# Planes of the experts' weight pieces, worked two slots later in the second attention

## The reference

```
h = _layernorm(x, ln1_g, ln1_b)
q = (h @ Wq).reshape(Bb, Ss, H, Dh); k = ...; v = ...
scores = jnp.einsum('bqhd,bkhd->bhqk', q, k) / jnp.sqrt(jnp.float32(Dh))
ctx = jnp.einsum('bhqk,bkhd->bqhd', jax.nn.softmax(scores, axis=-1), v)
x = x + ctx @ Wo
m = _layernorm(x, ln2_g, ln2_b)
probs = jax.nn.softmax(m @ Wg, axis=-1)
wts, idx = jax.lax.top_k(probs, K)
h1 = jax.nn.gelu(jnp.einsum('td,edf->etf', xt, W1) + b1[:, None, :])
ye = jnp.einsum('etf,efd->etd', h1, W2) + b2[:, None, :]
```

## Time and profile before

| | |
|---|---|
| median of 3 runs | 2354.14 us (2352.45 to 2356.22) |
| the profiled execution | 2354.95 us |
| its span | 2353.2 us |
| mean granted clock of TensorE | 0.904 |
| PE busy | 1868.1 us, 79% |
| DVE busy | 1611.5 us, 68% |
| ACT busy | 1474.4 us, 63% |

### The profile page before, as it was taken

The page is one execution under the profiler, slowest core; times in us unless marked ns, Lnnn a source line. Parts: engine busy times, 40 slices in busy tenths (PEclk is TensorE's granted clock), DMA queues, the critical chain, the costliest instruction groups (busy, mean ns, idle before and its releaser), DMA issues. The chain is left out here.

```text
span 2353.2 us, 39104 instructions
## 1 busy us (share of the span) xinstructions
PE 1868.1 (79%) x12343; PEld 1137.1 (48%) x12344; DVE 1611.5 (68%) x3496; ACT 1474.4 (63%) x2762; POOL 593.1 (25%) x638
## 2 busy tenths in 40 slices
PE   3577787878787877857998988898774699999990
PEld 1344554545454544532333333332223588888880
DVE  4488888888888888856766666666625555555556
ACT  1398989898998989951657666666562233333333
POOL 4331314141414050023101211210111233333320
PEclk9689999999999999987999999898885799999995
DMA  1221212121212121102111133443335511111116
GB/s 43 70 60 40 75 34 69 40 67 40 68 39 68 41 66 35 37 26 64 46 29 51 55 88 122 142 129 116 104 117 228 186 47 47 46 45 45 45 40 220
DMA packets 143652, 172.38 MB, mean 73 GB/s; under 512 B 27457, under 2 KB 123922, under 8 KB 141458
## 3 DMA queue, kind: packets, MB, share of 16 engines
q1 hardware_dynamic: 135010, 149.59, 20.9%
q0 software_dynamic: 7488, 20.46, 2.9%
q10 hardware_dynamic: 1008, 0.54, 0.1%
HBM read 105.47 MB, written 65.01 MB: 72 GB/s over the span
## 5 line engine op out<-in xcount | busy, mean ns | idle before, releaser
L1256 DVE TENSOR_REDUCE NM<-sP 128x1 f32<-128x512 f32 x512 | 332.4, 684 | 181.9 <-PE sP L1134 179.5
L1066 ACT ACTIVATE PT<-tP 128x512 f32<-128x512 f32 x512 | 286.4, 603 | 215.0 <-PE tP L1145 214.0
L478 ACT ACTIVATE YZ<-YZ,gsc 128x512 f32<-128x512 f32 (+3 forms) x512 | 341.9, 706 | 66.9 <-DVE YZ L665 66.9
L1502 ACT ACTIVATE H<-hP,B1T 128x256 f32<-128x256 f32 x312 | 127.2, 472 | 271.7 <-PE hP L1581 209.8
L676 DVE CUSTOM_DVE_ANT_0 YZ<-SeP,YZ 128x512 f32<-128x512 f32 (+3 forms) x512 | 238.9, 485 | 61.7 <-PE SeP L543 58.2
L542 PE MATMUL SeP<-SMV,SST 128*128 128x512 f16 (+3 forms) x512 | 162.6, 323 | 116.4 <-DVE mn L676 114.9
L1134 PE MATMUL sP<-STK,STQ 112*128 112x512 f16 x512 | 207.9, 408 | 32.7 <-DVE NM L1256 24.5
L1145 PE MATMUL tP<-STQ,STK 114*128 114x512 f16 x512 | 202.7, 402 | 35.4 <-ACT PT L1066 35.1
L456 ACT ACTIVATE XL<-mP 128x512 f32<-128x512 f32 (+1 forms) x384 | 219.7, 573 | 15.7 <-PE mP L553 15.6
L665 DVE SCALAR_TENSOR_TENSOR YZ<-YZ,XL 128x1280 f32<-128x1280 f32 x128 | 197.4, 1542 | 45.3 <-ACT YZ L470 45.0
L464 ACT ACTIVATE PTa<-tPa 128x512 f32<-128x512 f32 (+1 forms) x384 | 223.1, 581 | 5.8 <-PE tPa L574 5.0
(11 more groups left out here) (306 smaller groups left out, 4031.0 us busy)
## 6 DMA issues: line engine op xcount, KB each, us to landing
X<-in_L_ffn_W SPq DMA_DIRECT2D x32, 512.0 KB, 4.1
weight_planes<-X SPq DMA_DIRECT2D x64, 256.0 KB, 2.5
SST<-planes_a_scratch SPq DMA_DIRECT2D x384, 32.0 KB, 1.9
SMV<-planes_a_scratch SPq DMA_DIRECT2D x384, 32.0 KB, 1.8
planes_a_scratch<-HI SPq DMA_DIRECT2D x64, 128.0 KB, 1.7
planes_a_scratch<-LO SPq DMA_DIRECT2D x64, 128.0 KB, 1.8
Y<-results_scratch SPq DMA_DIRECT2D x16, 512.0 KB, 8.7
STQ<-planes_scratch SPq DMA_DIRECT2D x96, 64.0 KB, 2.6
```

The costliest lines, as they stand in the source:

```text
L478: act.activation(w, w, ACT.Square, bias=gsc[:, b % 2, 1, i, hh:hh + 1], scale=gsc[:, b % 2, 0, i, hh:hh + 1]).then_inc(hyp_ready, 1)
L1066: act.activation(PT[:, p % 4, par, kt, :], tP[x % 3][:, :], ACT.Exp).then_inc(exp_done, 1)
L1256: dve.tensor_reduce(NM[:, g % 2, col:col + 1], sP[n % 2][:, :], AX.X, ALU.max, negate=True).then_inc(max_done, 1)
```

## The change

The loads stay at base + 0. The high plane moves from base + 3 to base + 5, the low plane from base + 5 to base + 7, and the stores from base + 7 to base + 8.

```diff
@@ SP @@
                             sp.dma_start(WST.rearrange("p (k c) -> p k c", c=w.shape[2]), w).then_inc(wst_loaded, 16)
-                        k = at_piece(n, 7)
+                        k = at_piece(n, 8)
                         if k is not None:
                             w, plane, at = piece_of(k)
                             sp.wait_ge(w_low, k + 1)
@@ ACT @@
-                        k = at_piece(n, 3)
+                        k = at_piece(n, 5)
                         if k is not None:
                             act.wait_ge(wst_loaded, 16 * (k + 1))
@@ DVE @@
-                        k = at_piece(n, 5)
+                        k = at_piece(n, 7)
                         if k is not None:
                             dve.wait_ge(w_high, k + 1)
                             dve.scalar_tensor_tensor(WLO, WST, SCALE, WHI, ALU.mult, ALU.subtract).then_inc(w_low, 1)
```

## The result

The changed kernel takes 2334.86 us (median of 4 runs, 2330.48 to 2337.42) against 2353.3 us before (median of 4). The ratio is 0.9925, with a 95% interval of 0.9908 to 0.9941: 17.6 us faster, 13.9 to 21.7 at the ends of the interval (the two medians lie 18.4 us apart). The profiled execution has a span of 2333.9 us.

A forecast was written before the change was run, and what follows sets the result against it. PE bounds the second attention, with idle time and a slower clock where pieces load. Saving 9 us idle plus 5 us clock, 14 us, gave 2341 from 2354.95, set at 2340 us; forecast 2333 to 2348, 80% range 2323 to 2356.

The forecast's parts named there:

- The term for the clock: PE's clock falls to 0.50 after idle times; avoiding those at pieces 1 and 22 saves 5.7 us, rounded down to 5.
- Piece 1: PE idle 2.90 us, ACT waits 2.51 for the load; two slots less, 2.2 us saved.
- Piece 4: High plane between square root and table reload; first table load hidden in the wait, 3.2 us saved.
- Piece 11: PE idle 0.81 us; two slots more, but load 0.9 us later and tables right behind: 0 saved.
- Piece 18: PE idle 5.39 us; 0.9 us saved, the rest given to the table loads.
- Piece 22: PE idle 3.92 us; two slots, less a part at the slow clock: 2.0 us saved.
- Piece 25: PE idle 0.70 us of ACT's 2.19 us wait; load 0.9 later, high plane 2.4 later: 0.7 us saved.
- Piece 28: No other SP items ahead of its load, so it gains nothing and its wait stays.
- The low plane "counted at nothing": On DVE, two slots later delays the maximum as before, only in other slots; counted 0, at most 1.2 us at one place.
- Rival 3: Slower: high plane beside the square root keeps ACT from exps 4.0 us; four places could cost 23 us; chance 0.12.
- Rival 2: Hardly any change: PE's idle time only moves to the next wait, clock falls stay; 2350 to 2356 us; chance 0.22.
- Rival 1: More gain: all five clock falls go and remaining waits shrink; 23 to 35 us, about 2327 us; chance 0.13.

The follow-up runs named there:

- e8: Against kernel before: two load buffers from piece 8 on, loads issued at base - 5, planes and stores as before: ratio 0.9922.
- e3: Kernel before with low plane alone two slots later (base + 7) and stores at base + 8, high plane left at base + 3: ratio 0.9982.
- e10: Against kernel before: two load buffers from piece 8 on (loads at base - 5), high plane base + 5, low base + 7, stores base + 8: ratio 0.9888.
- e12: Against kernel before: two load buffers from piece 8, high plane base + 7, low and stores base + 9, from piece 8 base + 11 and + 12: ratio 0.9932.

## Why the prediction held, step by step

**The cause of the gain: right, and shown to be enough for it.** The load is late by its place in SP's queue. Moving the load two slots up (e4) or giving it another buffer (e8) gives the same gain as moving the planes two slots down (e2), and the stores' slot alone gives nothing that can be seen (e1). How much of the changed kernel's gain comes by the planes' places, by way of the wait for the maximum (e3), stays open. The load wait came out at 14.4 us, where 10 to 16 was forecast, and the four batches at 81.7 us each, where it was 82.

**The sum: right in total, wrong in its split.** 14 us were forecast as 9 of idle time and 5 of clock; the four batches show 5.4 and 9.9. Over the same slots in both kernels, 264 to 504, it is 7.2 and 10.8. The term for the clock was sized at half of what it was. It took two falls as avoided, at pieces 1 and 22, of the five behind waits for a piece. Before, the four batches have nine stretches at the lower level, 64.6 us in all; after, seven, 40.8 us. Two of those before, then two of those after:

```profile
1396.70:1403.50 6.80, 5.56 (x19) 1.01 (x22) 4.33 (x9) 3.87 (x8) 0.00 (x0) 0.50 0.24 80
1485.40:1492.20 6.80, 6.37 (x24) 1.41 (x26) 4.50 (x10) 3.67 (x8) 0.00 (x0) 0.50 0.31 99
```

```profile
1400.60:1404.00 3.40, 3.40 (x13) 0.56 (x12) 1.38 (x2) 1.19 (x2) 0.00 (x0) 0.50 0.87 292
1601.90:1612.10 10.20, 7.89 (x20) 4.54 (x21) 4.95 (x10) 7.16 (x12) 2.16 (x4) 0.50 0.32 103
```

The fall at piece 22 is gone. The one at piece 1 is halved (the first rows of the two), and the one at piece 4 is 6.8 us instead of 10.2. Those at pieces 11 and 18 grew from 6.8 to 10.2. Four falls of before, at 1485.4, 1509.3, 1594.6 and 1680.0, of 6.8 us each, stood at waits of 1.2 to 2.1 us for an exp, for `NMR` or for a maximum, and the sum had left them out; after, three such of 3.4 us are left. That makes 23.8 us less at the lower level. At the forecast's own price, 2.8 us for 6.8, it comes to 9.8, which is what was found (9.9).

**The terms, piece by piece.** ACT's high planes at pieces 1, 4, 11, 18 and 22 answer to the earlier trace rows (at piece 4 with the row that follows):

```profile
1397.22 1.06 ACT L1059 ACTIVATE X<-X 128x1024 f16<-128x1024 f32 x1 [1.06 <-DMA X<-in_L_ffn_W]
...
1432.90 1.06 ACT L1059 ACTIVATE X<-X 128x1024 f16<-128x1024 f32 x1 [1.60 <-DMA X<-in_L_ffn_W]
1433.98 1.28 ACT L1066 ACT_TABLE_LOAD   x1
...
1515.89 1.06 ACT L1059 ACTIVATE X<-X 128x1024 f16<-128x1024 f32 x1 [4.09 <-DMA X<-in_L_ffn_W]
...
1601.13 1.06 ACT L1059 ACTIVATE X<-X 128x1024 f16<-128x1024 f32 x1 [6.01 <-DMA X<-in_L_ffn_W]
...
1646.01 1.06 ACT L1059 ACTIVATE X<-X 128x1024 f16<-128x1024 f32 x1 [1.27 <-DMA X<-in_L_ffn_W]
```

and PE's idle times there to the earlier trace rows:

```profile
1399.39 1.07 PE L1169 MATMUL avPb<-PT,VS 128*32 128x512 f32 x8 [2.71 <-ACT PT L1066]
...
1435.93 0.61 PE L1145 MATMUL tP<-STQ,STK 114*128 114x512 f16 x1 [3.69 <-ACT PT L1066]
...
1517.97 1.11 PE L1177 MATMUL avPb<-ident,yT 128*128 128x128 f32 x4 [3.77 <-ACT yT L1072]
...
1602.72 0.61 PE L1145 MATMUL tP<-STQ,STK 114*128 114x512 f16 x1 [3.94 <-ACT PT L1066]
...
1607.21 0.61 PE L1145 MATMUL tP<-STQ,STK 114*128 114x512 f16 x1 [1.13 <-ACT PT L1066]
...
1647.61 0.39 PE L1145 MATMUL tP<-STQ,STK 114*128 114x512 f16 x1 [0.70 <-ACT PT L1066]
```

- Piece 1: 2.2 us of idle time were to go. ACT's wait fell from 2.51 to 1.06, but PE's idle time moved to the next `avPb` and is 2.71, against 2.90. This term failed in its place: the two slots ended in another wait for an exp. Over slots 264 to 296 idle time fell by 1.4 us.
- Piece 4: 3.2 was forecast from 3.18 + 1.13 turning into one wait that ends at 1435.4. It ends at 1435.93 (3.69 us), with the reload right behind the high plane, against slot 308 at 1438.61 before. In the trace of after the stage began 2.8 us later, so the gain is larger than these two numbers show. The sum by rows held here. Over slots 296 to 328 the kernel gained 3.7 us, 2.0 of it idle time. The Trainium skill ("ScalarE: Activation LUTs", section "What ACT_TABLE_LOAD costs") gives a drain of about 1.38 us with each switch of tables; by that, an estimate, the exp would have come 1.4 us later. The trace does not agree: the table load of 1.28 us begins 0.02 us after the high plane's end and is over at 1435.26, and PE has its buffer at 1435.93.
- Piece 11: 0 forecast. ACT waits 4.09 us instead of 2.94. PE's 3.77 and another 1.13 behind the table loads stand against 0.81, 0.99 and 1.12 before: 2.0 us more at the piece itself. The load was forecast 0.9 us late; e1 shows 1.2 us more of wait by the stores alone. PE came there earlier, with its wait at piece 10 gone (below); over slots 360 to 392 idle time is 6.8 us instead of 6.6.
- Piece 18: 0.9 forecast. The first wait is 3.94 instead of 5.39, but two more follow, 0.36 us for `yT` and 1.13 us at 1607.21 for the exp behind the table loads, which was not there before. Together 5.4 us as before. From slot 424 to slot 448 the kernel takes 37.1 us instead of 36.5. This term failed.
- Piece 22: 2.0 forecast; idle 0.70 instead of 3.92, 3.2 less, and the fall of the clock behind it is gone (granted clock 1.00 from 1640 to 1660 us).
- Piece 25: 0.7 forecast. ACT's wait of 2.19 us is gone; over slots 488 to 504 idle time is 4.3 us instead of 4.5. Nearly all of the 2.1 us gained there is busy time.
- Piece 28: nothing was to be gained there. Its wait of 1.34 us is gone all the same.

**The low plane "counted at nothing": right ahead of `NMR`, not for the maximum.** Before, PE stood 1.87 us at piece 10, where the low plane is the step ahead of `NMR` (timeline of before, DVE and PE):

```profile
1507.35 1.22 DVE L1248 SCALAR_TENSOR_TENSOR X<-X 128x1024 f16<-128x1024 f32 x1
...
1509.64 0.28 DVE L1265 TENSOR_TENSOR NMR<-nmf,NMR 16x128 f16<-16x128 f32 x1
...
1509.97 1.94 PE L1169 MATMUL avPb<-PT,VS 128*32 128x512 f32 x8 [1.87 <-DVE NMR L1265]
```

That idle time is gone at piece 10, and its twin is at piece 24 after:

```profile
1668.13 1.21 DVE L1248 SCALAR_TENSOR_TENSOR X<-X 128x1024 f16<-128x1024 f32 x1
...
1670.41 0.28 DVE L1265 TENSOR_TENSOR NMR<-nmf,NMR 16x128 f16<-16x128 f32 x1
...
1670.75 1.08 PE L1169 MATMUL avPb<-PT,VS 128*32 128x512 f32 x4 [1.87 <-DVE NMR L1265]
```

The same 1.87 us, only in another place. PE's wait for the maximum, however, fell from 15.0 to 10.1 us, and by the waits listed at e3 that goes with the low plane's slot. The sum had no term for it.

**The signs.** ACT's wait, PE's wait for an exp, the clock of the window (0.92) and the batch came out as named. That the clock "stays up after piece 1" did not: it is at 0.50 again from 1400.6 to 1404.0. A wait at piece 1 was left, which the forecast did not name, and that at piece 28 went, which it did.

**The rivals.** Rival 3, the square root, did not decide: at piece 4 PE's idle time fell. But the sign that it named, a new idle row with a table load ahead of it, came up at piece 18 (1.13 us at 1607.21). The 3.77 us at piece 11 are not such a row: they end at 1517.97, just as the first table load begins (1517.93). Rival 2, idle time that only moves, is what happened at pieces 1, 11 and 18, and in part in the whole: in the four batches PE's idle time ahead of `tP` fell from 23.7 to 15.6 us and ahead of `sP` from 15.6 to 11.4, but ahead of `avPb` it rose from 11.4 to 18.4. Rival 1 did not come about: 17.6 us are under its 23. It was right in that the clock could give back more than 5 us, and e10 shows that 26 us can be had with a second buffer (2353.22 x 0.0112).

**Where the theory is incomplete.** e3 (more load wait, yet faster) and e12 (nearly as little as e10, yet slower) show that the load wait doesn't fix the time. What PE's busy time goes with, over the same 256 slots, is the time at the lower level: 296.7 us busy with 64.6 at that level before, 289.9 with 47.6 in e3, 286.1 with 40.8 in the changed kernel, 286.7 with 44.2 in e12, 280.6 with 23.8 in e10. PE's idle time in these is 52.3, 52.7, 45.3, 39.8 and 39.0 us, so it does not fix that level. What decides it is open.

## What to carry to other kernels

When an engine waits for a DMA in a pipeline written out by slots, look at what stands ahead of that DMA in the issuing queue, not at its transfer: here 5.6 us of issuing stood against 4.1 us of landing. More slots between issue and use, an earlier place in the queue, or a second buffer were worth about the same here, and two of them together gave the fastest kernel. Count what a shorter wait does to TensorE's clock as a term of its own (here 9.9 us beside 5.4), look for all falls in the trace, those at short waits too, and judge it by PE's busy time for equal work: check that the two stretches hold the same slots.

## What was not expected of the hardware

For nearly the same matmuls (1396 and 1403) PE was busy between 276.0 us (e10) and 291.4 us (before) in the four batches, with the granted clock between 0.96 and 0.91. The clock fell to 0.50 not only at waits of 2.9 to 5.4 us: five of the nine falls before stood where no single wait of PE was over 2.1 us, the one at piece 11 behind waits of 0.8 and 1.0 us. And equal idle time does not give an equal clock: over the same 1425 matmuls, at 39.0 and 39.8 us idle, the clock was 0.96 in e10 and 0.93 in e12, worth 6.1 us.
